# Selective scan with one pass's inputs made on TensorE and a third output product on GpSimd

## The chip, the cores and the metric

The kernel runs on one core of a Trainium2 chip. The metric is the device time of one execution in microseconds (us). A core has five engines with a queue of instructions each: TensorE (PE, its weight loads shown as PEld), VectorE (DVE), ScalarE (ACT), GpSimd (POOL) and SyncE (SP), which here only issues transfers. They wait for one another by semaphores. SBUF is the on-chip memory; PSUM is the memory that TensorE writes and that GpSimd can't reach.

## The reference, cut to what matters

One block of a model on a sequence of 512 tokens of 512 channels: cross attention to a context of 8192 tokens, then a Mamba block with a gated MLP, then a mixture of experts. The change touches only the selective scan of the Mamba block:

```
delta = softplus(dt @ dt_proj_w.T + dt_proj_b)      # [512 tokens, 1024 channels]
A = -exp(A_log)                                     # [1024, 16 states]
def step(h, t):
    dA  = exp(delta_t[..., None] * A)
    dBx = (delta_t * x_t)[..., None] * B_t[:, None, :]
    h = dA * h + dBx
    y = einsum('bdn,bn->bd', h, C_t)
y = ys + xin * D
out = (y * silu(z)) @ out_proj_w.T
```

Everything here is float32, and channels lie on the 128 partitions.

## The kernel before, in words

`mamba_scan` works through 8 blocks of 128 channels (index f) and in each through 8 passes of 2 states (index q): 64 passes, numbered i. A pass has 2 x 512 elements per partition. Its steps:

- u = delta x xin for the block (128 x 512), once per block, on GpSimd (L1385) from the second block on.
- Inputs b = u x B: one product of 128 x 1024 on GpSimd (L1392) into a ring of RB = 3 buffers. B (`bb`) and C (`cc`) lie in SBUF, broadcast to all partitions. The very first is VectorE's (L1448).
- Decays: ScalarE sets the first column to 0 (L1405) and writes exp(delta x A) for each of the two states (L1408) into PSUM, `hs`, a ring of RS = 2.
- Scan: VectorE's tensor_tensor_scan (L1455), h = decay x h + input over the 1024 elements. It writes the states over the decays in PSUM, or, for the passes in `POOL_OUT` (1 and 4), into the SBUF buffer `hc`, ring of RC = 3.
- Output product h x C into `hc`: VectorE (L1462), for passes 1 and 4 GpSimd in place (L1380). GpSimd issues it after the inputs of two passes later.
- Sum: TensorE adds both states of `hc` into the PSUM bank `yp` by matmuls with the identity (L1516). The bank opens with the skip term xin x D (`xk`, L1513, made by ScalarE at L1414). At the end of a block VectorE multiplies the bank by silu(z) (`gate`, L1440), which it does after scan and product of pass 0 of the next block, and TensorE later does the out-projection (L1049), after the sum of pass 7 of the next block.

What sets the order: each engine runs its own list in the order of the code. VectorE's scan i waits for b (`b_ready`), for the decays (`da_ready`), and for the sum of pass i - 3 (`summed`, since the buffer of `hc` is used again). ScalarE's decays i wait until the states of pass i - 2 have been read: by VectorE's product, or for a pass of `POOL_OUT` by the scan alone (`wait_states`). GpSimd's product b waits for the scan of three passes before. TensorE's sums stand in order of i and wait for the product's engine (`wait_outputs`). In the first block ScalarE also does the Silu of z, after the decays of pass 3 (L1417). In the last block some out-projections stand after the sums of passes 2, 3 and 5 (`LAST_AT`).

Of the kernel before, what the change touches and what calls it, by code (L numbers as in the profile page):

```python
# [17 lines left out]
ALU = mybir.AluOpType  # L18
ACT = mybir.ActivationFunctionType
AX = mybir.AxisListType  # L20

P = 128
T = 512
D = 512
TT = T // P
# [1038 lines left out]
HN = 2  # L1064
PASSES = DS // HN

NOW_Z = 2

POOL_OUT = (1, 4)


def scan_rows(keep, first):
# [219 lines left out]
def mamba_scan(nc, keep, n2w, xd_dram, wpack, wsplit):  # L1292
# [6 lines left out]
    with ExitStack() as ctx:  # L1299
# [4 lines left out]
        b = [m.sb(f"b{i}", [P, HN, T]) for i in range(RB)]  # L1304
        hc = [m.sb(f"hc{i}", [P, HN, T]) for i in range(RC)]
        xk = m.sb("xk", [P, 2, T])
        squares = m.sb("squares", [P, 2, T])

        halves_of = lambda a, b: [t[:, 2 * (j % 4):2 * (j % 4) + 2, :].rearrange("p c n -> p (c n)").bitcast(F32)
                                  for j in range(DIC) for t in ((a, b)[j // 4],)]  # L1310
# [26 lines left out]
        block = ctx.enter_context(nc.Block())  # L1337
        passes = [(f, q) for f in range(DIC) for q in range(PASSES)]
        NP = len(passes)

        def pool_passes(n):
            return n // PASSES * len(POOL_OUT) + sum(q in POOL_OUT for q in range(n % PASSES))

        def wait_states(eng, i):

            if i % PASSES in POOL_OUT:
                eng.wait_ge(scanned, i + 1)
            else:
                eng.wait_ge(dve_hc, i + 1 - pool_passes(i))
# [7 lines left out]
        @block.sync  # L1357
        def _(sp):
            for q in range(PASSES):
                sp.dma_start(cc[q], xd_dram[DS + q * HN:DS + (q + 1) * HN, :].partition_broadcast(P)).then_inc(c_in[q], 16)  # L1360
            for n, place in enumerate((keep.hidden, keep.outl)):
                sp.dma_start(place.rearrange("p c n -> p (c n)").bitcast(F32),
                             wpack[W.OUT[0] + n:W.OUT[0] + n + 1, :, :].rearrange("o p n -> (o p) n")).then_inc(w_in, 16)
            sp.dma_start(nw[:, :], n2w).then_inc(n_in, 16)

            sp.wait_ge(b_ready, NP - 1)
            load_gates(sp, keep, wsplit, slice(0, DF // 2), next_in, (0,))
            sp.wait_ge(dve_hc, NP - pool_passes(NP))
            sp.wait_ge(pool_hc, pool_passes(NP))
            load_gates(sp, keep, wsplit, slice(0, DF // 2), next_in, (1,))  # L1370
            sp.wait_ge(next_in, 64)

        @block.gpsimd
        def _(pool):
            def output(i):
                q = i % PASSES
                pool.wait_ge(scanned, i + 1)
                if i < PASSES:
                    pool.wait_ge(c_in[q], 16)
                nc.gpsimd.tensor_tensor(hc[i % RC][:, :, :], hc[i % RC][:, :, :], cc[q], ALU.mult).then_inc(pool_hc, 1)  # L1380

            for i, (f, q) in enumerate(passes):
                if q == 0 and f:
                    pool.wait_ge(b_ready, i - 1)
                    nc.gpsimd.tensor_tensor(u[:, :], keep.delta[:, f, :], keep.xin[:, f, :], ALU.mult).then_inc(u_ready, 1)  # L1385
                    pool.wait_ge(u_ready, f)
                if i >= RB:
                    pool.wait_ge(scanned, i - RB + 1)
                if i == 1:
                    pool.wait_ge(first_ready, 1)  # L1390
                if i:
                    nc.gpsimd.tensor_tensor(b[i % RB][:, :, :], u[:, :].unsqueeze(1).to_broadcast([P, HN, T]),  # L1392
                                            bb[q], ALU.mult).then_inc(b_ready, 1)
                if i >= RB - 1 and (i - RB + 1) % PASSES in POOL_OUT:
                    output(i - RB + 1)
            for i in range(NP - RB + 1, NP):
                if i % PASSES in POOL_OUT:
                    output(i)

        @block.scalar  # L1400
        def _(act):
            for i, (f, q) in enumerate(passes):
                if i >= RS:
                    wait_states(act, i - RS)
                nc.scalar.activation(hs[:, i % RS, :, 0], zero[:, :], ACT.Copy)  # L1405
                for n in range(HN):
                    s = q * HN + n
                    last = nc.scalar.activation(hs[:, i % RS, n, 1:], keep.delta[:, f, 1:], ACT.Exp,  # L1408
                                                scale=aneg[:, f, s:s + 1])
                last.then_inc(da_ready, 1)  # L1410
                if q == 0:
                    if f >= 2:
                        act.wait_ge(summed, PASSES * (f - 2) + 1)
                    nc.scalar.activation(xk[:, f % 2, :], keep.xin[:, f, :], ACT.Copy,  # L1414
                                         scale=dk[:, f:f + 1]).then_inc(xk_ready, 1)
                if i == 3:
                    nc.scalar.activation(keep.zs[:, NOW_Z:, :], keep.zs[:, NOW_Z:, :], ACT.Silu).then_inc(zs_ready, 1)  # L1417

            nc.scalar.activation(rows.sd[:, 0:HN], zero[:, :], ACT.Sqrt).then_inc(warm, 1)
            act.wait_ge(warm, 1)  # L1420
            for t in range(TT):
                act.wait_ge(sum_ready, t + 1)
                if t >= 2:
                    act.wait_ge(ss_ready, t - 1)
                nc.scalar.activation(squares[:, t % 2, :], keep.a[:, t, :], ACT.Square,
                                     accum_out=ss[:, t:t + 1]).then_inc(ss_ready, 1)
            act.wait_ge(var_ready, 1)
            nc.scalar.activation(rows.sd[:, :], rows.var[:, :], ACT.Sqrt).then_inc(sd_ready, 1)
            act.wait_ge(nws_ready, 1)
            for c in range(DC):  # L1430
                act.wait_ge(hT_ready, c + 1)
                nc.scalar.activation(keep.hh[:, c, :], hT[c], ACT.Copy, scale=nws[:, c:c + 1]).then_inc(hh_ready, 1)

        @block.vector
        def _(dve):
# [6 lines left out]
            for i, (f, q) in enumerate(passes):  # L1442
                h = hs[:, i % RS, :, :]
                flat = h.rearrange("p n t -> p (n t)")
                if i:
                    dve.wait_ge(b_ready, i)
                else:
                    nc.vector.tensor_tensor(b[0][:, :, :], u[:, :].unsqueeze(1).to_broadcast([P, HN, T]),  # L1448
                                            bb[0], ALU.mult).then_inc(first_ready, 1)
                    dve.wait_ge(first_ready, 1)  # L1450
                dve.wait_ge(da_ready, i + 1)
                if i >= RC:
                    dve.wait_ge(summed, i - RC + 1)
                out = hc[i % RC][:, :, :]
                nc.vector.tensor_tensor_scan((out if q in POOL_OUT else h).rearrange("p n t -> p (n t)"), flat,  # L1455
                                             b[i % RB].rearrange("p n t -> p (n t)"), 0.0,
                                             ALU.mult, ALU.add).then_inc(scanned, 1)
                if q not in POOL_OUT:
                    dve.wait_ge(scanned, i + 1)
                    if f == 0:  # L1460
                        dve.wait_ge(c_in[q], 16)
                    nc.vector.tensor_tensor(out, h, cc[q], ALU.mult).then_inc(dve_hc, 1)  # L1462
                if q == 0 and f:
                    gate(f - 1)
                if f == DIC - 1 and q == 1:
                    dve.wait_ge(early_ready, 1)
                    nc.vector.tensor_tensor(keep.a[:, 0, :], early, keep.a[:, 0, :], ALU.add).then_inc(early_read, 1)
# [24 lines left out]
        def _(pe):  # L1492
            def out_proj(j, ts):

                pe.wait_ge(y_ready, j + 1)
                for t in ts:
# [8 lines left out]
                    if j == DIC - 1:  # L1505
                        last.then_inc(o_ready, 1)

            for i, (f, q) in enumerate(passes):
                if q == 0:
                    if f:  # L1510
                        pe.wait_ge(y_ready, f)
                    pe.wait_ge(xk_ready, f + 1)
                    nc.tensor.matmul(yp[:, :], ident[:, :], xk[:, f % 2, :], start=True, stop=False)  # L1513
                wait_outputs(pe, i)
                for n in range(HN):
                    last = nc.tensor.matmul(yp[:, :], ident[:, :], hc[i % RC][:, n, :],  # L1516
                                            start=False, stop=(q == PASSES - 1 and n == HN - 1))
                last.then_inc(summed, 1)
                if q == 7 and f:
                    if f == 1:  # L1520
                        pe.wait_ge(w_in, 32)
                    out_proj(f - 1, range(TT - 1) if f - 1 < EARLY else range(1, TT))
                if f == DIC - 1 and q in LAST_AT:
                    pe.wait_ge(early_read, 1)
                    for j in LAST_AT[q]:
                        out_proj(j, (TT - 1,))
# [816 lines left out]
```

## Time and profile before

| what | value |
|---|---|
| median of 3 runs | 2522.21 us (2520.57 to 2522.47) |
| profiled execution, its own time | 2526.3 us |
| its span, first to last instruction | 2524.4 us |
| mean granted TensorE clock | 0.983 |
| the scan stage, from its first instruction to the last gate | 1879.6 to 2091.3 us |
| busy, whole span: PE, DVE, ACT, POOL | 2398.6, 1974.6, 1601.7, 669.9 us |

A busy time counts instructions of an engine from start to end. The granted clock of TensorE is a share of 2.4 GHz; 0.50 is 1.2 GHz. A timeline row merges neighbouring instructions of one line: start, time that they cover, engine, line, operation, out<-in, shapes, count; the bracket is the idle time of the engine before it and who ended it.

### The profile page before, as it was taken

The numbers are of one execution on the slowest core, as the hardware profiler recorded it, in microseconds if no ns is written. First come the engines' busy times: TensorE is split into PE (matmuls) and PEld (weight loads), VectorE is DVE, ScalarE is ACT, GpSimd is POOL, SyncE is SP. The second block draws the span as 40 slices with busy tenths as digits, with TensorE's granted clock in tenths as the row PEclk, the third lists the DMA queues.
The fourth block names the chain that finished last, engine by engine and source line by source line (L and its number), as shares of the span: only waits on it lengthen the run. The fifth ranks groups of instructions, "written<-read, shape, count | busy, mean of one in ns | idle before, by whom it ended". The sixth has DMA issues, their size and how long they took to land. (4 is left out here: it accounts for less than half of the span.)

```text
span 2524.4 us, 39338 instructions
## 1 busy us (share of the span) xinstructions
PE 2398.6 (95%) x14111; PEld 1016.1 (40%) x14111; DVE 1974.6 (78%) x1972; ACT 1601.7 (63%) x1974; POOL 669.9 (27%) x461
## 2 busy tenths in 40 slices
PE   7999999999999799999999999999887778989998
PEld 3333333333333244444444444444332234444554
DVE  5777777777777788888988898988679993267996
ACT  5555555565555478777778877778384442237994
POOL 1455555555555400000000000000019990020001
PEclk9999999999999899999999999999989999999999
DMA  6245654455445593433334333433240005148994
GB/s 250 84 151 164 204 164 150 158 173 167 150 137 157 137 264 81 114 100 98 104 88 110 90 104 88 112 97 95 102 158 22 0 0 200 50 176 317 406 406 171
DMA packets 178206, 366.02 MB, mean 145 GB/s; under 512 B 19546, under 2 KB 90330, under 8 KB 174426
## 3 DMA queue, kind: packets, MB, share of 16 engines
q1 hardware_dynamic: 176610, 360.81, 44.8%
q0 software_dynamic: 1280, 4.20, 0.5%
q8 instruction: 38, 0.62, 0.1%
q14 instruction: 30, 0.24, 0.0%
q10 hardware_dynamic: 248, 0.15, 0.0%
HBM read 254.24 MB, written 106.68 MB: 143 GB/s over the span
## 5 line engine op out<-in xcount | busy, mean ns | idle before, releaser
L466 DVE TENSOR_REDUCE kv_mx<-kv_s 128x1024 f32 (+1 forms) x512 | 595.3, 1217 | 223.7 <-PE kv_s L502 223.7
L818 DVE TENSOR_TENSOR at_pl<-at_pf,at_ph 128x1024 f16<-128x1024 f32 x512 | 613.1, 1223 | 115.6 <-ACT at_ph L765 106.7
L771 ACT ACTIVATE at_pf<-at_st 128x1024 f32<-128x1024 f32 x512 | 497.3, 1025 | 190.3 <-PE at_st L939 137.5
L938 PE MATMUL at_st<-keep_big,at_k_cur 128*128 (+1 forms) x1024 | 390.6, 381 | 10.1 <-DMA keep_big<-q_dram 7.3
L939 PE MATMUL at_st<-keep_big,at_k_one 128*128 (+1 forms) x1024 | 389.1, 380 | 0.0
L765 ACT ACTIVATE at_ph<-at_pf 128x1024 f16<-128x1024 f32 x256 | 272.9, 1066 | 0.0
L1135 POOL MEMSET mamba_zero<- 128x2 f32 x1 | 0.1, 99 | 943.7 <-POOLq L60 943.7
L900 PE MATMUL at_acc<-at_ph,at_vs 128*128 128x512 f16 x1024 | 243.0, 380 | 3.4 <-DVE at_pl L818 3.3
L382 POOL TENSOR_TENSOR kv_ksl<-kv_kf,kv_ksh 128x512 f16<-128x512 f32 x128 | 147.9, 1156 | 247.4 <-ACT kv_ksh L410 247.4
L1049 PE MATMUL kv_kp<-first_ch,first_wkh 128*128 128x512 f16 x512 | 195.4, 382 | 6.1 <-DVEq L448 6.1
L407 ACT ACTIVATE kv_kf<-kv_kp,first_bks 128x512 f32<-128x512 f32 x128 | 87.3, 682 | 172.6 <-PE kv_kp L1049 172.6
L1049 PE MATMUL kv_kp<-first_ch,first_wkl 128*128 128x512 f16 x512 | 195.4, 382 | 0.0
L1049 PE MATMUL kv_kp<-first_cl,first_wkh 128*128 128x512 f16 x512 | 195.1, 381 | 0.0
L1049 PE MATMUL kv_vp<-first_wvh,first_ch 128*128 128x512 f16 x512 | 194.7, 380 | 0.3 <-DVE kv_mx L466 0.3
L1049 PE MATMUL kv_vp<-first_wvl,first_ch 128*128 128x512 f16 x512 | 194.6, 380 | 0.0
L1049 PE MATMUL kv_vp<-first_wvh,first_cl 128*128 128x512 f16 x512 | 194.2, 379 | 0.0
L414 ACT ACTIVATE kv_vf<-kv_vp 128x512 f32<-128x512 f32 x128 | 76.0, 594 | 184.8 <-PE kv_vp L1049 184.8
L386 POOL TENSOR_TENSOR kv_vs<-kv_vf,kv_vs 128x512 f16<-128x512 f32 x128 | 147.9, 1155 | 130.0 <-ACT kv_vs L416 130.0
L814 DVE CAST at_ph<-at_pf 128x1024 f16<-128x1024 f32 x256 | 177.6, 694 | 0.0
L1516 PE MATMUL ms_yp<-ms_hc,keep_ident 128*128 128x512 f32 x256 | 131.7, 655 | 47.6 <-POOL ms_hc L1380 32.7
L938 PEld LDWEIGHTS at_st<-keep_big,at_k_cur 128*128 128x128 f16 x1024 | 100.2, 98 | 171.9 <-issue 54.8
L1392 POOL TENSOR_TENSOR ms_b<-mamba_u,keep_big 128x1024 f32<-128x1024 f32 x63 | 146.4, 2351 | 55.5 <-DVE ms_b L1448 55.0
(349 smaller groups left out, 3863.3 us busy)
## 6 DMA issues: line engine op xcount, KB each, us to landing
keep_big<-gate_up SPq DMA_DIRECT2D x17, 2048.0 KB, 13.0
at_vs<-vd SPq DMA_DIRECT2D x64, 512.0 KB, 3.9
at_k_cur<-kd SPq DMA_DIRECT2D x126, 256.0 KB, 3.8
vd<-kv_vs SPq DMA_DIRECT2D x15, 2048.0 KB, 7.7
kv_tf<-wpack SPq DMA_DIRECT2D x21, 1024.0 KB, 6.3
keep_big<-down SPq DMA_DIRECT2D x17, 1024.0 KB, 14.0
first_cf<-ctxT SPq DMA_DIRECT2D x16, 1024.0 KB, 12.2
ex_yg<-gate_up SPq DMA_DIRECT2D x8, 2048.0 KB, 13.6
```

What stands on the lines that cost most here:

```text
L382: nc.gpsimd.tensor_tensor(ksl[par][:, n, :], kf[:, n % 4, :], ksh[par][:, n, :], ALU.subtract).then_inc(kl_ready, 1)
L386: nc.gpsimd.tensor_tensor(vs[par][:, hs, kt, DH:2 * DH], vf[:, n % 4, :].rearrange("p (h d) -> p h d", d=DH), vs[par][:, hs, kt, 0:DH], AL ...
L466: nc.vector.reduce_max(mx[:, bass.ds(g * (NH * TT) + 2 * (m - TT), 2)], s1[:, m % 3, :, :], AX.X).then_inc(s1_max, 1)
L765: nc.scalar.activation(ph[:, s % RING, :, :], pf[:, s % FULL, :, :], ACT.Copy).then_inc(ph_ready, 1)
L771: nc.scalar.activation(pf[:, s % FULL, :, :], st[:, s % HP % NST, :, :], ACT.Exp, scale=SCORE).then_inc(pf_ready, 1)
L814: nc.vector.tensor_copy(ph[:, s % RING, :, :], pf[:, s % FULL, :, :]).then_inc(ph_own, 1)
L818: nc.vector.tensor_tensor(pl[:, s % RING, :, :], pf[:, s % FULL, :, :], ph[:, s % RING, :, :], ALU.subtract).then_inc(pl_ready, 1)
L900: nc.tensor.matmul(acc[:, 0, :], vs[:, 2 * s + e, :], ph[:, s % RING, e, :], start=(s == 0 and e == 0), stop=False)
L938: nc.tensor.matmul(st[:, w % NST, e, :], k_cur[:, tile], qh[:, q], start=True, stop=False)
L939: last = nc.tensor.matmul(st[:, w % NST, e, :], k_one[:, tile], ql[:, q], start=False, stop=True)
L1049: last = nc.tensor.matmul(out, a, b, start=(start and n == 0), stop=(stop and n == len(pairs) - 1))
L1392: nc.gpsimd.tensor_tensor(b[i % RB][:, :, :], u[:, :].unsqueeze(1).to_broadcast([P, HN, T]), bb[q], ALU.mult).then_inc(b_ready, 1)
```

## The change

- `POOL_OUT` becomes (1, 4, 6): the output product of pass 6 goes from VectorE to GpSimd, and its scan writes `hc`.
- Pass 7 (`TE_PASS`) of each block has its inputs made by TensorE, in PSUM, and no longer by GpSimd. `turn(f)`: four transposes write u of the block, turned, into the half of a state buffer of pass 3 (`TURN_AT`) before its decays go there; ScalarE copies it to SBUF (`uT`). `inputs(f)`: eight matmuls of 128 x 128 x 128 with `uT` as weights and `dg`, B's two rows of pass 7 on diagonals, as the moving side write u x B into `hs`. `turn` stands in TensorE's order ahead of the sum of pass 1, `inputs` ahead of the sum of pass 4.
- The decays of pass 7 go to an SBUF buffer `da`. Its scan reads decays from SBUF and inputs from PSUM.
- VectorE makes `dg` once, by two products after the scan of pass 2.
- GpSimd's and VectorE's counts of `b_ready` leave pass 7 out; GpSimd waits for `turned` before it writes the next u; the squares of the row norm after the scan use the buffer `xk`.

```diff
-POOL_OUT = (1, 4)
+POOL_OUT = (1, 4, 6)
+TE_PASS, TURN_AT = 7, 3
...
-        squares = m.sb("squares", [P, 2, T])
+        squares = xk
+        uT, dg, da = m.sb("uT", [P, TT, P]), m.sb("dg", [P, HN, TT, P]), m.sb("da", [P, HN, T])
...
+        def pool_inputs(n):
+            return n // PASSES * (PASSES - 1) + min(n % PASSES, TE_PASS)
...
 # sync
-            sp.wait_ge(b_ready, NP - 1)
+            sp.wait_ge(b_ready, pool_inputs(NP) - 1)
...
 # gpsimd
-                    pool.wait_ge(b_ready, i - 1)
+                    pool.wait_ge(b_ready, pool_inputs(i) - 1)
+                    pool.wait_ge(turned, f)
...
-                if i >= RB:
-                    pool.wait_ge(scanned, i - RB + 1)
+                k = pool_inputs(i)
+                if q != TE_PASS and k >= RB:
+                    pool.wait_ge(scanned, ITS_PASS[k - RB] + 1)
...
-                if i:
-                    nc.gpsimd.tensor_tensor(b[i % RB][:, :, :], u[:, :].unsqueeze(1).to_broadcast([P, HN, T]),
+                if i and q != TE_PASS:
+                    nc.gpsimd.tensor_tensor(b[k % RB][:, :, :], u[:, :].unsqueeze(1).to_broadcast([P, HN, T]),
                                             bb[q], ALU.mult).then_inc(b_ready, 1)
...
 # scalar
-                if i >= RS:
+                if q == TE_PASS:
+                    if f:
+                        act.wait_ge(scanned, i - PASSES + 1)
+                elif i >= RS:
                     wait_states(act, i - RS)
-                nc.scalar.activation(hs[:, i % RS, :, 0], zero[:, :], ACT.Copy)
+                if q == TURN_AT:
+                    act.wait_ge(turned, f + 1)
+                    if f:
+                        act.wait_ge(in_ready, f)
+                    nc.scalar.activation(uT.rearrange("p t d -> p (t d)"), hs[:, i % RS, 0, :], ACT.Copy).then_inc(uT_ready, 1)
+                    act.wait_ge(uT_ready, f + 1)
+                decays = da if q == TE_PASS else hs[:, i % RS, :, :]
+                nc.scalar.activation(decays[:, :, 0], zero[:, :], ACT.Copy)
...
 # vector
-                if i:
-                    dve.wait_ge(b_ready, i)
+                if q == TE_PASS:
+                    dve.wait_ge(in_ready, f + 1)
+                elif i:
+                    dve.wait_ge(b_ready, pool_inputs(i))
...
+                if q == TE_PASS:
+                    decays, inputs = da.rearrange("p n t -> p (n t)"), flat
+                else:
+                    decays, inputs = flat, b[pool_inputs(i) % RB].rearrange("p n t -> p (n t)")
...
+                if i == 2:
+                    for n in range(HN):
+                        nc.vector.tensor_tensor(dg[:, n, :, :], bb[TE_PASS][:, n, :].rearrange("p (t c) -> p t c", c=P),
+                                                ident[:, :].unsqueeze(1).to_broadcast([P, TT, P]),
+                                                ALU.mult).then_inc(dg_ready, 1)
...
 # tensor
+            def turn(f):
+                i = f * PASSES + TURN_AT
+                wait_states(pe, i - RS)
+                if f:
+                    pe.wait_ge(u_ready, f)
+                for t in range(TT):
+                    last = nc.tensor.transpose(hs[:, i % RS, 0, t * P:(t + 1) * P], u[:, t * P:(t + 1) * P], ident[:, :])
+                last.then_inc(turned, 1)
+
+            def inputs(f):
+                i = f * PASSES + TE_PASS
+                wait_states(pe, i - RS)
+                pe.wait_ge(uT_ready, f + 1)
+                if f == 0:
+                    pe.wait_ge(dg_ready, HN)
+                for t in range(TT):
+                    for n in range(HN):
+                        last = nc.tensor.matmul(hs[:, i % RS, n, t * P:(t + 1) * P], uT[:, t, :], dg[:, n, t, :],
+                                                start=True, stop=True)
+                last.then_inc(in_ready, 1)
...
             for i, (f, q) in enumerate(passes):
+                if q == TURN_AT - 2:
+                    turn(f)
+                if q == TE_PASS - 3:
+                    inputs(f)
```

## Rows read from the trace of the kernel before

**Rows 1.** Stretches: engine, busy us and count in 26 us of the scan; PEclk, DMA.

```profile
1956.00:1982.00 26.00, 19.52 (x44) 7.60 (x43) 25.79 (x16) 12.05 (x27) 24.68 (x12) 1.00 0.00 0
```

**Rows 2.** Timeline, VectorE, one block: start us, us, engine, line, operation, count.

```profile
1961.49 1.22 DVE L1462 TENSOR_TENSOR ms_hc<-ms_hs,keep_big 128x1024 f32<-128x1024 f32 x1
...
1962.63 0.68 DVE L1440 TENSOR_TENSOR mamba_yh<-ms_yp,mamba_zs 128x512 f32<-128x512 f32 x1
...
1963.23 2.28 DVE L1455 TENSOR_TENSOR_SCAN ms_hc<-ms_hs,ms_b 128x1024 f32<-128x1024 f32 x1
...
1965.43 2.27 DVE L1455 TENSOR_TENSOR_SCAN ms_hs<-ms_hs,ms_b 128x1024 f32<-128x1024 f32 x1
...
1967.73 1.22 DVE L1462 TENSOR_TENSOR ms_hc<-ms_hs,keep_big 128x1024 f32<-128x1024 f32 x1
...
1968.88 2.29 DVE L1455 TENSOR_TENSOR_SCAN ms_hs<-ms_hs,ms_b 128x1024 f32<-128x1024 f32 x1
...
1987.23 1.22 DVE L1462 TENSOR_TENSOR ms_hc<-ms_hs,keep_big 128x1024 f32<-128x1024 f32 x1
```

**Rows 3.** Groups by line, GpSimd, one block: count, busy us, mean ns, idle.

```profile
L1392 POOL TENSOR_TENSOR ms_b<-mamba_u,keep_big 128x1024 f32<-128x1024 f32 x9 | 20.9, 2352 | 0.1
...
L1385 POOL TENSOR_TENSOR mamba_u<-mamba_delta,mamba_xin 128x512 f32<-128x512 f32 x1 | 1.3, 1266 | 0.1
```

**Rows 4.** Timeline, GpSimd, its first product with C; in brackets idle before, releaser.

```profile
1965.59 2.34 POOL L1380 TENSOR_TENSOR ms_hc<-ms_hc,keep_big 128x1024 f32<-128x1024 f32 x1 [1.16 <-DVE ms_hc L1455]
```

**Rows 5.** Tile of the output sum: the matmul records of L1516.

```profile
L1516 PE MATMUL ms_yp<-ms_hc,keep_ident x256: 592/592/1223, 1884.7 to 2090.0; 128*128 128x512 f32 x128
```

**Rows 6.** Timeline, TensorE, sums of passes 0 and 1 before.

```profile
1964.56 1.88 PE L1516 MATMUL ms_yp<-ms_hc,keep_ident 128*128 128x512 f32 x4
...
1965.42 0.19 PEld L1516 LDWEIGHTS ms_yp<-ms_hc,keep_ident 128*128 128x128 f32 x1 [0.24 <-issue]
```

**Rows 7.** Timeline, last sum and final gate of the scan.

```profile
2088.60 1.98 PE L1516 MATMUL ms_yp<-ms_hc,keep_ident 128*128 128x512 f32 x4 [0.81 <-DVE ms_hc L1462]
...
2090.62 0.69 DVE L1440 TENSOR_TENSOR mamba_yl<-ms_yp,mamba_zs 128x512 f32<-128x512 f32 x1 [2.08 <-PE ms_yp L1516]
```

**Rows 8.** Timeline, float32 transposes of 128 columns: full clock, then 1.2 GHz.

```profile
2304.21 0.57 PEld L2183 LDWEIGHTS ex_up<-keep_ident,ex_smf 128*128 128x128 f32 x4
...
2304.43 0.60 PE L2183 MATMUL ex_up<-keep_ident,ex_smf 128*128 128x128 f32 x4
...
2102.27 2.42 PEld L1533 LDWEIGHTS ms_hs<-keep_ident,ms_hc 128*128 128x128 f32 x12 [5.65 <-issue]
```

**Rows 9.** Timeline, TensorE, pass 4's sum in the block f = 2.

```profile
1951.47 4.97 PE L1516 MATMUL ms_yp<-ms_hc,keep_ident 128*128 128x512 f32 x7 [2.75 <-POOL ms_hc L1380]
...
1952.42 0.34 PEld L1516 LDWEIGHTS ms_yp<-ms_hc,keep_ident 128*128 128x128 f32 x1 [0.52 <-issue]
```

**Rows 10.** Stretch in that sum, with its granted clock (PEclk).

```profile
1952.00:1953.00 1.00, 1.00 (x2) 0.34 (x1) 1.00 (x2) 0.64 (x2) 1.00 (x1) 0.50 0.00 0
```

**Rows 11.** Lines L1157 (ScalarE reads PSUM) and L1225 (VectorE, both inputs in SBUF).

```profile
L1157 ACT ACTIVATE mi_xp<-mi_zp x8: 578/581/598, 1830.1 to 1849.1; 128x512 f32<-128x512 f32 x8
...
L1225 DVE TENSOR_TENSOR mamba_u<-mamba_delta,mamba_xin x1: 682/682/682, 1877.5 to 1877.5; 128x512 f32<-128x512 f32 x1
```

**Rows 12.** Timeline, ScalarE, zero column and decays of one pass.

```profile
1962.75 0.17 ACT L1405 ACTIVATE ms_hs<-mamba_zero 128x2 f32<-128x2 f32 x1 [2.07 <-DVE ms_hc L1462]
...
1962.86 1.28 ACT L1408 ACTIVATE ms_hs<-mamba_delta,mamba_aneg 128x511 f32<-128x511 f32 x2
```

**Rows 13.** Timeline, first block: sum 0, decays of passes 3 and 4, scan 4.

```profile
1884.72 3.78 PE L1516 MATMUL ms_yp<-ms_hc,keep_ident 128*128 128x512 f32 x4 [0.98 <-DVE ms_hc L1462]
...
1887.01 1.28 ACT L1408 ACTIVATE ms_hs<-mamba_delta,mamba_aneg 128x511 f32<-128x511 f32 x2
...
1893.73 1.30 ACT L1408 ACTIVATE ms_hs<-mamba_delta,mamba_aneg 128x511 f32<-128x511 f32 x2
...
1895.11 2.29 DVE L1455 TENSOR_TENSOR_SCAN ms_hc<-ms_hs,ms_b 128x1024 f32<-128x1024 f32 x1 [1.34 <-ACT ms_hs L1408]
```

More of the change, by code:

```diff
@@ L1306, in mamba_scan @@
         xk = m.sb("xk", [P, 2, T])
-        squares = m.sb("squares", [P, 2, T])
+        squares = xk
+        uT, dg, da = m.sb("uT", [P, TT, P]), m.sb("dg", [P, HN, TT, P]), m.sb("da", [P, HN, T])
+        turned, uT_ready, dg_ready, in_ready = (m.sem(n) for n in ("turned", "uT_ready", "dg_ready", "in_ready"))
         halves_of = lambda a, b: [t[:, 2 * (j % 4):2 * (j % 4) + 2, :].rearrange("p c n -> p (c n)").bitcast(F32)
@@ L1339, in mamba_scan @@
         NP = len(passes)
+        ITS_PASS = [i for i, (f, q) in enumerate(passes) if q != TE_PASS]
         def pool_passes(n):
             return n // PASSES * len(POOL_OUT) + sum(q in POOL_OUT for q in range(n % PASSES))
+        def pool_inputs(n):
+            return n // PASSES * (PASSES - 1) + min(n % PASSES, TE_PASS)
         def wait_states(eng, i):
@@ L1402, in _ @@
             for i, (f, q) in enumerate(passes):
-                if i >= RS:
+                if q == TE_PASS:
+                    if f:
+                        act.wait_ge(scanned, i - PASSES + 1)
+                elif i >= RS:
                     wait_states(act, i - RS)
-                nc.scalar.activation(hs[:, i % RS, :, 0], zero[:, :], ACT.Copy)
+                if q == TURN_AT:
[6 more added lines that the diff above has]
+                nc.scalar.activation(decays[:, :, 0], zero[:, :], ACT.Copy)
                 for n in range(HN):
                     s = q * HN + n
-                    last = nc.scalar.activation(hs[:, i % RS, n, 1:], keep.delta[:, f, 1:], ACT.Exp,
+                    last = nc.scalar.activation(decays[:, n, 1:], keep.delta[:, f, 1:], ACT.Exp,
                                                 scale=aneg[:, f, s:s + 1])
@@ L1454, in _ @@
                 out = hc[i % RC][:, :, :]
-                nc.vector.tensor_tensor_scan((out if q in POOL_OUT else h).rearrange("p n t -> p (n t)"), flat,
-                                             b[i % RB].rearrange("p n t -> p (n t)"), 0.0,
-                                             ALU.mult, ALU.add).then_inc(scanned, 1)
+                if q == TE_PASS:
+                    decays, inputs = da.rearrange("p n t -> p (n t)"), flat
+                else:
+                    decays, inputs = flat, b[pool_inputs(i) % RB].rearrange("p n t -> p (n t)")
+                nc.vector.tensor_tensor_scan((out if q in POOL_OUT else h).rearrange("p n t -> p (n t)"), decays, inputs,
+                                             0.0, ALU.mult, ALU.add).then_inc(scanned, 1)
+                if i == 2:
[3 more added lines that the diff above has]
+                                                ALU.mult).then_inc(dg_ready, 1)
                 if q not in POOL_OUT:
```

## The prediction

> **What bounds the kernel now.** I read the table of stretches first. In the 26 us stretch of the scan stage VectorE is busy 25.79 us and GpSimd 24.68, ScalarE 12.05 [rows 1]: VectorE has no gap, GpSimd a little, ScalarE half. So the scan's time is what VectorE issues, and only what VectorE does or waits for counts. The timeline of one block of 128 channels (f = 3 into f = 4) gives its cadence, start to start [rows 2]: a scan and its multiply 3.45 us (1965.43 to 1968.88: scan 2.30, multiply 1.15), a scan whose output GpSimd multiplies 2.20 (1963.23 to 1965.43), the gate multiply 0.60. One block is 6 x 3.45 + 2 x 2.20 + 0.60 = 25.7 us, and the rows of the two multiplies with C at 1961.49 and 1987.23 are 25.74 apart. Eight blocks are the stage, from 1879.6 to the last gate.
>
> GpSimd makes per block eight products u x B of 2.35 us, one u of 1.27 [rows 3] and two products with C of 2.34; before the first of these it sits idle 1.16 us, waiting for a scan [rows 4]. At 2.3 us start to start its own work is 24.6 us.
>
> **The change, part by part.**
>
> *Removed.* VectorE no longer multiplies pass 6: 3.45 becomes 2.25; with the shorter handover of a scan that follows a scan, 2.20. That is 1.26 us less per block, 10.1 in eight. GpSimd exchanges one product of 2.35 for one of 2.34, so its 24.6 stay. If VectorE ran free at 25.74 - 1.26 = 24.5, GpSimd's 24.6 would be the bound, and the gain at most 1.1 per block.
>
> *Added on TensorE, and its place.* This is the step that decides. Inputs of pass 7 are eight plain float32 products of 128 columns, issued ahead of pass 4's sum in TensorE's program. They wait until VectorE has multiplied pass 5, since they overwrite that state. Queued behind them is the sum of pass 4, and the scan of pass 7 waits for this sum as well (the ring of three outputs: pass 7 needs passes 0 to 4 summed). In the kernel before, pass 4 is summed as soon as GpSimd has its product, well ahead of need. Now a chain runs from the end of pass 5's multiply: 0.06 to start, the eight products, the sum of 1.98, 0.04 to VectorE. Beside it runs only the scan of pass 6: by the cadence scan 7 could start 2.12 us after pass 5's multiply ends (multiply 1.22 long, next scan 1.14 after its start, next one 2.20 later). The old multiply of pass 6, which would have covered 1.26 more, is gone.
>
> How long are the eight? The view by tile lists 256 matmul records for the 128 sums' matmuls [rows 5]: a plain float32 matmul is two records, so sixteen records of 128 columns. For 512 columns a record takes 0.427 us (four in 1.88 with a tail of 0.17; the sum takes 1.98 in all [rows 6, 7]). By columns 128 are 0.107, the lower bound: 1.7 us for sixteen. Upper bound: a weight load of 0.19 [rows 6] not hidden at all, 0.30 each, 4.8 us. The nearest rows are float32 transposes: four loads in 0.57 with 0.14 the last, 0.143 apart, at the full clock; twelve in 2.42, 0.20 apart, with the clock at 1.2 GHz [rows 8]. A plain load record is longer (0.19 against 0.14). I take 0.17 at 2.4 GHz: 2.7 us. The stall of scan 7 is 0.06 + 2.7 + 1.98 + 0.04 - 2.12 = 2.7 us.
>
> The clock makes it worse. Before its sum of pass 4 TensorE sits idle 2.75 us, and the granted clock falls to 0.50 (1.2 GHz) right there: at 1951.8 it starts the sum and the rows after it show 0.50 and loads of 0.34 [rows 9, 10]. The same fall stands at this place in five of the eight blocks (0, 2, 4, 5, 6), some 3.5 us each. The new wait is at this place, idle longer still (until pass 5's multiply), so I let five of eight groups of products run at 1.2 GHz, with the 0.17 stretched as the transposes' 0.143 to 0.20: 0.24, sixteen 3.8 us, stall 3.8; the sum behind it again at 2.4. Together 3 x 2.7 + 5 x 3.8 = 27.1 us.
>
> *The rule on loads.* The loads of the sums start while the previous matmul streams and are followed by 0.24 us of waiting [rows 6]: hidden. The Trainium skill, "TensorE: Matmul & The Clock Gate", Part 3, "The mechanism", says the opposite for full-height tiles: a weight load overlaps matmuls in flight only if the row groups differ. Its "LDWEIGHTS" section gives 128 columns / 1.2 = 107 ns; an estimate from this page is 0.107 + 0.107 per record, a stall of 3.4 in each block, and by that a sum of 22 us where my 2.7 gives 16, both with the clock up. The rows speak against it for long matmuls and show nothing for plain short ones.
>
> *Turning u.* Four transposes between the sums of pass 0 and 1, then ScalarE copies them out of PSUM, waits for its own copy, and only then makes the decays of pass 3. Before, these could begin at the end of scan 1. Counted from the gate's start G = 1962.63: TensorE is busy with out-projection, the skip term and sum 0 until G + 3.64 (last record 1965.42 + 0.43, the rest being the pipeline), so the transposes end at G + 4.27 (0.60 for four [rows 8]); copy 0.58 [rows 11], own wait 0.04; zero column to first decay 0.11, decays 1.28 [rows 12]: ready at G + 6.35. Scan 3 starts at G + 6.25 (1968.88). So 0.1 per block, 0.6 in the six blocks that have an out-projection there; ScalarE's idle half covers the rest. Without that cover each further microsecond would be one of stall.
>
> *First block.* With the clock at 1.2 GHz sum 0 takes 3.78 us from 1884.72, its stream ending at 1888.1 [rows 13]; transposes 1.0, copy 0.6, and decays of pass 3 end at 1891.2 instead of 1888.3. Behind them ScalarE has the Silu of z with its table loads; so pass 4's decays end at 1897.9 instead of 1895.03, and scan 4, which already waits for them (1.34 idle), starts 2.8 later. The two diagonal products of VectorE (128 x 512, both inputs in SBUF, 0.68 each [rows 11]) lie inside these 2.8 and cost nothing more. Without that cover the two would cost VectorE 1.3.
>
> *Last block.* Sum 5, an out-projection of two matmuls, sum 6 and sum 7 are four times 1.71 behind the late sum 4, so the final gate, which waits 2.08 for sum 7 today [rows 7], waits about 1.2 more.
>
> *At nothing:* decays of pass 7 into SBUF (ScalarE need not wait for a state any more; it runs them right after pass 6's); the extra semaphores; the earlier weight load on SyncE's queue (bytes that the next stage needs 10 us later); the shared buffer of squares (used after the scan). GpSimd's wait for the turn ends long before it computes u. GpSimd's third product with C ends about as sum 4 does and its sum is needed only by the gate some 7 us later.
>
> **Sum:** -10.1 + 27.1 + 0.6 + 2.8 + 1.2 = +21.6 us. The profiled execution took 2526.3 (its span 2524.4), 4.1 above the median of 2522.2; the difference laid on the median gives 2543.8. A block should last 25.74 - 1.26 + 2.7 or 3.8 + 0.1 = 27.3 to 28.4.
>
> **Rivals.**
> A. The loads of short float32 matmuls are not hidden: 0.30 each hot, stall 4.8; cold 0.34 + 0.21 = 0.55, stall 8.8. All hot: -10.1 + 38.4 + 4.6 = +33, 2555; with the five falls +53, 2575. For it: nothing here streams short plain float32 products. Against: hidden loads in the rows of the sums, and transposes at less than load plus stream. The Trainium skill's rule quoted above is this rival's mechanism.
> B. The products cost half: one record each as the sixteen transposes have (0.107, 0.86 in all): stall 0.8, sum -10.1 + 6.6 + 4.6 = +1.1, 2523: no change. Against: two records per plain matmul.
> C. Faster: sum 4 does not hold scan 7, because the products are done before VectorE gets there, and GpSimd's 24.6 sets the block: 8 x -1.14 + 2.8 + 0.6 = -5.7, 2516.5. It decides from the point where sixteen records and the sum fit into 2.12 us; as the sum alone is 1.98, this needs TensorE's order or waits to be other than I read them. Break-even is at (10.1 - 4.6) / 8 = 0.7 us of stall.
> That the change doesn't do what it says, with the output of pass 6 left on VectorE, I see no sign of.
>
> **Chances.** Forecast 0.67, A 0.15, B 0.08, C 0.10. The forecast's own range: records at 0.107 and no falls give +8 (2530), all eight at 1.2 GHz and 0.19 for 0.17 give +29: 2530 to 2551. The range for 8 in 10 takes in B's edge and A's lower part: 2522 to 2560. What can be told from no change is 0.2%, 5 us. Slower 0.82, same 0.08, faster 0.10.
>
> **What would show it.** VectorE idle before the scan of pass 7 in every block, released by TensorE's sum, 2.5 to 4 us each; sixteen short records right ahead of the four of sum 4; a block of 27.3 to 28.4; GpSimd with 3 us idle per block; scan 4 of the first block near 1898. Wrong if scan 7 follows scan 6 at 2.20 us, if the eight products take under 1 us, or if GpSimd is the engine without gaps.

## The result, and the profile after

The changed kernel takes 2549.87 us (median of 5 runs, 2547.78 to 2551.99) against 2522.47 before (5 runs): ratio 1.0102, 95% interval 1.0091 to 1.0113, slower by 27.4 us. 2543.8 was predicted, with 2522 to 2560 as the range. The profiled executions took 2550.1 and 2526.3, 23.8 apart; the one of before lay 3.8 above its median, the one of after on it. I measure by the stage, from VectorE's first product to the final gate: 211.0 us before (1879.60 to 2090.62), 234.2 after (1878.75 to 2112.99), so 23.2 of the 23.8 are in it. Blocks, gate to gate, last 27.9 to 28.2 us in four cases, 29.3 in two and 26.8 in the last one; before they last 25.7, and 25.0 the last one.

VectorE's waits in the stage after the change (who waited for whom: us in total, times, longest), the answer to [rows 2]; before, VectorE had none ahead of the scan of pass 7:

```profile
DVE ms_hs L1483 <- PE ms_yp L1573: 27.6, 8, 4.6
DVE mamba_yl L1462 <- PE ms_yp L1573: 3.2, 1, 3.2
```

And the timeline of VectorE in one block: scan 5, its multiply, scan 6, scan 7.

```profile
1983.56 2.27 DVE L1483 TENSOR_TENSOR_SCAN ms_hs<-ms_hs,ms_b 128x1024 f32<-128x1024 f32 x1
1985.87 1.23 DVE L1494 TENSOR_TENSOR ms_hc<-ms_hs,keep_big 128x1024 f32<-128x1024 f32 x1
1987.01 2.28 DVE L1483 TENSOR_TENSOR_SCAN ms_hc<-ms_hs,ms_b 128x1024 f32<-128x1024 f32 x1
1993.88 2.30 DVE L1483 TENSOR_TENSOR_SCAN ms_hs<-ms_da,ms_hs 128x1024 f32<-128x1024 f32 x1 [4.59 <-PE ms_yp L1573]
```

Scan 6 follows pass 5's multiply by 1.14 as before; scan 7 should follow 2.20 later, at 1989.2, and starts at 1993.88. TensorE in the same stretch, the answer to [rows 9]: sixteen short records, then the sum of pass 4 (merged here with the next one); and the same two in the last block.

```profile
1987.15 3.78 PE L1557 MATMUL ms_hs<-ms_dg,ms_uT 128*128 128x128 f32 x16 [3.66 <-DVE ms_hc L1494]
1990.72 3.46 PE L1573 MATMUL ms_yp<-ms_hc,keep_ident 128*128 128x512 f32 x5
```

```profile
2102.31 2.05 PE L1557 MATMUL ms_hs<-ms_dg,ms_uT 128*128 128x128 f32 x16 [1.88 <-DVE ms_hc L1494]
2104.20 3.17 PE L1573 MATMUL ms_yp<-ms_hc,keep_ident 128*128 128x512 f32 x7
```

The stretches (PE busy, PEld, DVE, ACT, POOL, then PEclk) say why the first took 3.78 us and the other 2.05:

```profile
1988.00:1989.00 1.00, 1.00 (x6) 1.00 (x6) 1.00 (x1) 0.00 (x0) 1.00 (x1) 0.50 0.00 0
1992.00:1993.00 1.00, 1.00 (x2) 0.34 (x1) 0.00 (x0) 0.00 (x0) 1.00 (x2) 0.50 0.00 0
2103.00:2104.00 1.00, 1.00 (x12) 1.00 (x11) 1.00 (x1) 0.10 (x1) 0.00 (x0) 1.00 1.05 377
```

At 1.2 GHz the sum too is slow: from 1990.72 to 1993.88 it is 3.2 us instead of 2.0. The granted clock fell at this place in seven of the eight blocks. TensorE sat idle 3.6 to 3.7 us before the products in these seven and 1.9 us in the last, where the clock stayed up. In four of the seven it fell in the idle time (in the block shown at 1986.2), in three of them 0.4 to 1.3 us after the products had begun. VectorE's wait before scan 7 follows it: 1.76 us with the clock up, 3.15 to 3.44 in the five blocks where it was down for some 3.5 us, 4.53 and 4.59 in the two where it was down for some 7.

### The profile page after: what moved, and what is told of

It reads as the page before. It is cut to its first block and busy times, and to the rows that moved or that the text cites. A ratio compares the mean times of both kernels' runs of the same rounds, so it can differ in the third digit from the quotient of the medians.

```text
span 2548.2 us, 39690 instructions
## 1 busy us (share of the span) xinstructions
PE 2422.2 (95%) x14271; PEld 1042.7 (41%) x14271; DVE 1969.9 (77%) x1966; ACT 1607.3 (63%) x1982; POOL 672.9 (26%) x461
## 5 line engine op out<-in xcount | busy, mean ns | idle before, releaser
L900 PEld LDWEIGHTS at_acc<-at_ph,at_vs 128*128 128x128 f16 x1024 | 99.9, 98 | 124.4 <-DVE at_pl L818 4.5
L1403 POOL TENSOR_TENSOR ms_b<-mamba_u,keep_big 128x1024 f32<-128x1024 f32 x55 | 129.2, 2369 | 73.1 <-DVE ms_b L1472 56.3
```

The costliest lines, as they stand in the source:

```text
L900: nc.tensor.matmul(acc[:, 0, :], vs[:, 2 * s + e, :], ph[:, s % RING, e, :], start=(s == 0 and e == 0), stop=False)
L1403: nc.gpsimd.tensor_tensor(b[k % RB][:, :, :], u[:, :].unsqueeze(1).to_broadcast([P, HN, T]), bb[q], ALU.mult).then_inc(b_ready, 1)
```

## The experiments

All times are medians beside runs of the kernel before on the same chip (2522.5 to 2523.9); "stage" as above. The numbers (e1 to e11) are those by which the expectations name one another: "the second experiment" is e2, "the tenth" e10.

**e1: the order of products and sum 4.**

```diff
-                if q == TE_PASS - 3:
+                if q == TE_PASS - 2:
                     inputs(f)
```

> The eight products of pass 7 stand behind the sum of pass 4 in TensorE's order instead of ahead of it; nothing else changes. Theory (the scan of pass 7 waits for a chain of products and sum that starts at the end of pass 5's multiply): sum 4 can now start when GpSimd's product is done, 0.9 us before that multiply ends, so the chain is shorter by that: a wait of scan 7 of 0.9 us where the clock is up and 2.6 where it falls before sum 4, about 16 us in eight blocks where there were 27.6; time about 2538. Rival (GpSimd's third product with C is what is late, the order on TensorE doesn't matter): the waits stay at 3 to 4 us, time 2550.

2535.1 us, ratio 1.0045 (1.0028 to 1.0062); stage 220.6. The waits before scan 7 fell by half and name the products now, no sum:

```profile
DVE ms_hs L1483 <- PE ms_hs L1557: 13.5, 8, 2.4
```

So 13.7 us of the stage were one line of order: the chain is shown. Part of them came by the clock: like with like, the wait is 0.64 us for 1.76 with the clock up and about 2.3 for 3.3 with it down, some 1.1 us per block either way; the rest is that the clock now fell at this place in five blocks, not seven, and never for 7 us.

**e3: the length of the products.** In `inputs`, `for n in range(HN)` becomes `for n in range(1)`. This kernel leaves out half of the inputs of pass 7.

> Leaves out four of the eight products of each block (the second state of pass 7 keeps what was in PSUM). Theory with length in it: 0.94 us less per block with the clock up, 1.8 with it down, the sum of the waits before scan 7 falls from 27.6 to 14 to 18 us, time about 2537. Rival (the wait is a matter of order and handovers, the length of the products is small beside it): under 4 us less.

```profile
DVE ms_hs L1483 <- PE ms_yp L1573: 16.5, 8, 2.5
```

2538.4 us in its one run, near the 2537 expected. 11.1 us of waiting less for eight times eight records less is 0.17 us each, but some of it is the clock again, which fell at this place in six blocks and never for 7 us. In the last block, at full clock in both kernels, the wait is 0.87 for 1.76: 0.11 us a record.

**e7: the clock.** `none` holds zeros, written by GpSimd at the start (that line isn't shown).

```diff
             def inputs(f):
                 i = f * PASSES + TE_PASS
+                if f == 0:
+                    pe.wait_ge(none_ready, 1)
+                for n in range(4):
+                    nc.tensor.matmul(yp[:, :], none[:, :], cc[0][:, 0, :], start=False, stop=False)
                 wait_states(pe, i - RS)
```

> Four matmuls of 512 columns with zero weights are added into the output sum just ahead of TensorE's wait for pass 5's multiply (3.4 us of work in an idle time of 3.7), so that TensorE isn't idle before the products. Theory: the granted clock stays at 2.4 GHz through products and sum 4, sixteen records take 1.9 us as in the one block where it was up, each wait is 1.8 us as there, sum about 15 us where it was 27.6; time 2537. Rival (the clock is no part of it, the products are slow by themselves): waits stay at 3 to 4.5 us, time 2550 or, with the filler late, more.

2536.5 us, ratio 1.0049 (1.0032 to 1.0065), stage 223.7. Waits and, in one block, the products:

```profile
DVE ms_hs L1487 <- PE ms_yp L1581: 15.4, 8, 3.1
```

```profile
1955.30 2.05 PE L1565 MATMUL ms_hs<-ms_dg,ms_uT 128*128 128x128 f32 x16 [0.23 <-DVE ms_hc L1498]
```

With work ahead of them the products run as in the last block of the changed kernel (2.05 us), and 12.2 of 27.6 us of waiting are gone, though TensorE does more; the stage is 10.5 shorter. Seven of the eight waits are now 1.76 us, that of the block whose clock had stayed up; in the last block the wait grew to 3.1, as the added work (3.4 us) is longer than TensorE's idle time there (1.9). The granted clock is 1.00 in all eight groups of products and the sums behind them. So of the time lost at this place nearly half was the granted clock, and TensorE's idle time before the products was what brought it down.

**e5, one part alone: the inputs on TensorE.** `POOL_OUT` back to (1, 4).

> The changed kernel with pass 6's output product back on VectorE (two passes on GpSimd as before), inputs of pass 7 still on TensorE. Theory: the 1.26 us per block of that product now lie beside TensorE's products and sum 4 and cover them; the waits of scan 7 shrink by as much, from 27.6 to about 18 us in all, and the time is that of the changed kernel within a few us: 2547 to 2552. That would say that moving the product to GpSimd bought nothing here. Rival (each part has its own cost or gain, the move gains 10 us by itself): 2560.

2549.8 us, ratio 1.0106 (1.0089 to 1.0123), no different from the changed kernel's. The waits:

```profile
DVE ms_hs L1483 <- PE ms_yp L1573: 17.3, 8, 3.3
```

10.3 us less than 27.6, which is the 10.1 of work that came back. The product's move to GpSimd bought nothing: it uncovered the wait.

**e4, one part alone: the third product on GpSimd.** The kernel before with `POOL_OUT = (1, 4, 6)`.

> The kernel before with the output product of pass 6 on GpSimd and nothing else: GpSimd makes all eight inputs and three output products. Theory (work of GpSimd's list, 8 x 2.32 + 3 x 2.30 + 1.45): GpSimd has 26.9 us of work per block and becomes the bound, blocks of 26.9 to 27.2 instead of 25.74, stage from 211.0 to about 221, time 2532. Rival (VectorE's released time counts, GpSimd keeps up through its rings): blocks of 24.5 to 25, time 2515.

2543.9 us, ratio 1.0078 (1.0061 to 1.0094), stage 232.6; both theories missed. VectorE waits, at the gates:

```profile
DVE mamba_yh L1440 <- PE ms_yp L1516: 17.0, 4, 4.7
DVE mamba_yl L1440 <- PE ms_yp L1516: 15.2, 4, 4.7
```

GpSimd's work, 26.9 us per block, is part of it; the rest is order: its product of pass 6 stands behind u and the next block's first inputs, sums 6 and 7 come after it, and the gate waits up to 4.7 us. Behind the late gate stands the scan of pass 1, and for this GpSimd in turn sits idle, 1.54 or 2.78 us by turns:

```profile
1973.30 2.35 POOL L1380 TENSOR_TENSOR ms_hc<-ms_hc,keep_big 128x1024 f32<-128x1024 f32 x1 [1.54 <-DVE ms_hc L1455]
```

26.87 and these give the blocks of 28.4 and 29.6 us that alternate here.

**e6: four output buffers.** `RB, RC, RS = 3, 4, 2`.

> The changed kernel with four output buffers instead of three, so that the scan of pass 7 needs passes 0 to 3 summed and no longer pass 4. Theory: only the products themselves (1.9 us with the clock up, about 3.6 down, and 0.3 of latency) can hold scan 7, beside 2.12 of cover: waits of 0.1 to 1.9, 8 to 12 us in all instead of 27.6; time 2530 to 2534. Rival (the sum behind the products doesn't matter, scan 7 waits for the products anyway): waits stay above 20 us, 2545 or more.

2543.0 us, ratio 1.0077 (1.0060 to 1.0094); stage 227.7. Its waits:

```profile
DVE ms_hs L1483 <- PE ms_hs L1557: 8.5, 7, 1.7
DVE ms_hs L1483 <- ACT ms_hs L1430: 5.9, 5, 1.4
DVE mamba_yl L1462 <- PE ms_yp L1573: 5.0, 1, 5.0
...
DVE mamba_yh L1462 <- PE ms_yp L1573: 3.0, 4, 1.0
DVE ms_hs L1483 <- POOL ms_b L1403: 2.1, 2, 1.4
```

The products hold scan 7 for 8.5 us in all, as expected of the one wait. The time missed the expectation by 10 us: once scan 7 isn't late, sums 4 to 7, the out-projection and the turning of u are still late on TensorE. They hold the gates (8.0 us, 5.0 of it the last one) and, by the decays of pass 3, scan 3 (1.4 us in each of four blocks). Taking one wait away moved VectorE into the next.

**e2: pass 6 on TensorE.** `TE_PASS = 6`, products behind sum 3.

> Pass 6 instead of pass 7 gets its inputs from TensorE; the state that these overwrite is pass 4's, which is free as soon as scan 4 ends, since GpSimd multiplies that pass; the products stand behind sum 3. Theory: scan 5 and its multiply (3.45 us) now cover the products (1.9 us with the clock up, 3.6 with it down), so VectorE's waits before that scan nearly vanish (under 0.5 us each, 0.2 in most), a block lasts about GpSimd's 24.6 to 24.9 us instead of 28.3, and the time is 2517 to 2523, on either side of the kernel before. Rival (GpSimd with three products with C, or short products on TensorE as such, cost the time): blocks stay above 27 us and the time above 2540.

2555.3 us, ratio 1.0127 (1.0110 to 1.0144), stage 245.4: the slowest of all. Where I had aimed, the theory holds; scan 5, its multiply and scan 6 follow without a gap:

```profile
1985.14 2.27 DVE L1483 TENSOR_TENSOR_SCAN ms_hs<-ms_hs,ms_b 128x1024 f32<-128x1024 f32 x1
...
1987.45 1.22 DVE L1494 TENSOR_TENSOR ms_hc<-ms_hs,keep_big 128x1024 f32<-128x1024 f32 x1
...
1988.59 2.27 DVE L1483 TENSOR_TENSOR_SCAN ms_hc<-ms_da,ms_hs 128x1024 f32<-128x1024 f32 x1
```

But the gates wait 34 us in all:

```profile
DVE mamba_yh L1462 <- PE ms_yp L1573: 16.9, 4, 4.8
DVE mamba_yl L1462 <- PE ms_yp L1573: 16.9, 4, 4.7
```

The reason is GpSimd's list (inputs of pass 7, u, inputs of pass 0, product of pass 6):

```profile
1957.81 2.36 POOL L1403 TENSOR_TENSOR ms_b<-mamba_u,keep_big 128x1024 f32<-128x1024 f32 x1
1960.25 1.27 POOL L1395 TENSOR_TENSOR mamba_u<-mamba_delta,mamba_xin 128x512 f32<-128x512 f32 x1
1961.59 2.34 POOL L1403 TENSOR_TENSOR ms_b<-mamba_u,keep_big 128x1024 f32<-128x1024 f32 x1
1963.90 2.34 POOL L1389 TENSOR_TENSOR ms_hc<-ms_hc,keep_big 128x1024 f32<-128x1024 f32 x1
```

Scan 6 ended at 1961.07; its product starts at 1963.90, after u and the inputs. Time and blocks (up to 30.7 us) are as the rival has them, but not by its cause: with the same three products in another order, in e9, they aren't.

**e9: the same with GpSimd's list put right.** It makes the inputs of pass 7 before it multiplies pass 4:

```diff
-                if i >= RB - 1 and (i - RB + 1) % PASSES in POOL_OUT:
-                    output(i - RB + 1)
+                late = i - (3 if q == PASSES - 1 else 2)
+                if q != TE_PASS and late >= 0 and late % PASSES in POOL_OUT:
+                    output(late)
```

> Pass 6 gets its inputs from TensorE behind sum 3, as in the second experiment, and GpSimd makes the inputs of pass 7 before it multiplies pass 4 by C (there it sat idle 3.6 us waiting for scan 4, and its product of pass 6 came so late that the gate waited 3.7 to 4.8 us per block, 33.8 in all). Theory: product of pass 6 ends about 8.4 us after scan 4, sums 6 and 7 at 12.2, the gate is due at 12.6: the gate's waits fall under 1 us where the clock is up, blocks take 24.6 to 25.2, stage about 205, time 2516 to 2520, faster than the kernel before. Rival (the gate waits because sums 6 and 7 run at 1.2 GHz or stand behind other work of TensorE): waits of 2 us and more remain, blocks above 26, time above 2528.

2527.9 us (ratio 1.0017, 1.0007 to 1.0027), 27 us better than without it, stage 213.3; blocks of 25.7, not 24.6, so it isn't faster than the kernel before, though I had expected that. Only the first gate (1.3 us) and the last (2.9) still wait. What was left is in neither theory: scan 3 waits 1.13 to 1.26 us in five blocks for the decays behind the copy of u.

```profile
1968.94 0.60 PE L1547 MATMUL ms_hs<-keep_ident,mamba_u 128*128 128x128 f32 x4
...
1969.62 0.60 ACT L1425 ACTIVATE ms_uT<-ms_hs 128x512 f32<-128x512 f32 x1 [3.86 <-DVE ms_hs L1484]
...
1971.73 2.30 DVE L1484 TENSOR_TENSOR_SCAN ms_hs<-ms_hs,ms_b 128x1024 f32<-128x1024 f32 x1 [1.15 <-ACT ms_hs L1431]
```

**e10: the out-projection later**, so that TensorE turns u earlier: blocks 2 to 6 do it behind the sum of pass 2.

> As the last experiment of pass 6 on TensorE with GpSimd's new order, and in blocks 2 to 6 the out-projection stands behind the sum of pass 2 instead of behind the sum of pass 7 of the block before. There TensorE's turning of u came after the out-projection, and scan 3 waited 1.15 us per block for decays behind the copy of u. Theory: turned u is there 2.6 us earlier, that wait goes in five blocks, blocks of 24.55 to 24.7 (GpSimd's 24.6), stage from 213.3 to about 208, time 2520 to 2522. Rival (the wait comes from ScalarE's own order, copy and its wait before the decays, whatever TensorE does): blocks stay at 25.7, time 2527.

2522.6 us, ratio 0.9997 (0.9988 to 1.0006): no change against the kernel before. The stage is 209.7, not 208. The wait at scan 3 is gone in the five blocks, and GpSimd is the engine without gaps in the middle ones: its inputs of pass 0 in two following blocks are 24.44 apart. Two of the seven blocks still last 26.0 us: there the granted clock fell to 0.50 in sums 6 and 7, and the gate behind them waits 1.46.

```profile
1957.34 2.35 POOL L1403 TENSOR_TENSOR ms_b<-mamba_u,keep_big 128x1024 f32<-128x1024 f32 x1
...
1981.78 2.35 POOL L1403 TENSOR_TENSOR ms_b<-mamba_u,keep_big 128x1024 f32<-128x1024 f32 x1
```

**e8: the diagonal products.**

> The changed kernel with the two diagonal products of VectorE at the very start of the scan, while GpSimd still waits for its first buffer, instead of after scan 2, where they took 2.13 us each. Theory (they are slow because GpSimd works beside them on SBUF while both their inputs are in SBUF): 0.68 us each here. Rival (their access pattern, a row against an identity repeated four times, is slow by itself): 2.1 each here too. The stage's start is later by the products' time either way; time 2550 to 2552.

2551.0 us in one run. Each product takes 0.69 us here, so the theory holds and their access pattern isn't what is slow. By tile (ns: least, median, greatest), in the changed kernel and here:

```profile
L1487 DVE TENSOR_TENSOR ms_dg<-keep_big,keep_ident x2: 1514/2170/2827, 1888.4 to 1889.8; 128x512 f32<-128x512 f32 x2
```

```profile
L1465 DVE TENSOR_TENSOR ms_dg<-keep_big,keep_ident x2: 684/688/691, 1877.5 to 1878.1; 128x512 f32<-128x512 f32 x2
```

**e11: first block.** On top of e10, the turn of block 0 goes before pass 5, and `dg` reads the identity from PSUM.

> The tenth experiment, and in the first block u is turned before pass 5 and not before pass 3, so that ScalarE's Silu isn't behind the copy; and the diagonal products read the identity from PSUM (a transpose of TensorE puts it there), so one of their inputs only is in SBUF, with GpSimd working beside them. Theory: diagonal products of 0.68 us instead of 2.13, scan 4 of the first block 2.5 to 3.3 us earlier, some 0.6 given back at scan 5: stage about 205.5, time 2518 to 2520. Rival (their access pattern is slow by itself): 2.1 each, scan 4 is then bound by them, time as in the tenth.

```profile
L1490 DVE TENSOR_TENSOR ms_dg<-keep_big,ms_op x2: 674/674/674, 1887.8 to 1888.4; 128x512 f32<-128x512 f32 x2
```

```profile
1893.98 2.29 DVE L1485 TENSOR_TENSOR_SCAN ms_hc<-ms_hs,ms_b 128x1024 f32<-128x1024 f32 x1 [0.29 <-ACT ms_hs L1432]
```

With GpSimd working beside them and one input in PSUM the products take 0.67 us, and scan 4 starts 15.6 us into the stage, where it was 18.4 in e10, as expected.

2520.0 us, ratio 0.9991 (0.9982 to 1.0000), stage 206.4, 4.6 below the kernel before. The stage is clearly shorter; of the whole the runs can't tell more than 0 to 0.2%. It is the best version, and no clear win.

## Why the prediction was right

- *The deciding step held*: products, then sum 4, then scan 7, from the end of pass 5's multiply. Waits of 27.6 us (28.2 with the handover, 0.08 more each) against 27.1 predicted. That the sum came so close is luck: two errors cancel. Products at the full clock were cheaper: (2104.20 - 2102.31) / 16 = 0.118 us a record, near my lower bound of 0.107, where I took 0.17. The clock fell in seven blocks, not five, and stayed down for some 7 us in two of them, so that sum 4 ran slow as well; I had given the falls to the products alone. Against my 3 x 2.7 + 5 x 3.8 stand 1 x 1.76, five waits of 3.15 to 3.44 and two of 4.5: no single block waited what I said, and two blocks of 29.3 us and the last of 26.8 lie outside my 27.3 to 28.4. I also read the fall of the clock before the change as coming ahead of the sum of pass 4, with the sum starting at 1951.8; the row has it start at 1951.47, and the clock fell at 1951.6.
- *Removed work*: 10.1. Without its wait the block after the first lasts 27.97 - 3.41 - 0.08 = 24.48 (from 1908.50 to 1936.47).
- *Turning u*: 0.1 predicted in six blocks (the terms add up to G + 6.28, not 6.35), 0.2 measured in five: in the last block VectorE has an addition to do ahead of scan 2, and nothing waits. In the five, scan 3 starts 1.34 after the multiply and not 1.14, behind the decays:

```profile
1975.78 0.60 ACT L1424 ACTIVATE ms_uT<-ms_hs 128x512 f32<-128x512 f32 x1 [2.82 <-issue]
...
1976.52 1.28 ACT L1430 ACTIVATE ms_hs<-mamba_delta,mamba_aneg 128x511 f32<-128x511 f32 x2
1976.55 1.22 DVE L1494 TENSOR_TENSOR ms_hc<-ms_hs,keep_big 128x1024 f32<-128x1024 f32 x1
...
1977.89 2.30 DVE L1483 TENSOR_TENSOR_SCAN ms_hs<-ms_hs,ms_b 128x1024 f32<-128x1024 f32 x1
```

- *First block*: 2.8 predicted; scan 4 starts 18.4 us into the stage instead of 15.5, so 2.9. ScalarE's chain did what was forecast (decays ready at 1896.92), but the diagonal products took 4.3 us and not 1.4. VectorE has no gap from them to scan 4, so they alone made scan 4 as late. With them out of the way, in e8, scan 4 waits 3.2 us for ScalarE and starts as late. That the 2.8 fits is luck too, since I had these products three times too cheap:

```profile
1888.35 4.26 DVE L1487 TENSOR_TENSOR ms_dg<-keep_big,keep_ident 128x512 f32<-128x512 f32 x2
...
1895.62 1.30 ACT L1430 ACTIVATE ms_hs<-mamba_delta,mamba_aneg 128x511 f32<-128x511 f32 x2
...
1897.13 2.28 DVE L1483 TENSOR_TENSOR_SCAN ms_hc<-ms_hs,ms_b 128x1024 f32<-128x1024 f32 x1
```

- *Last gate*: it waits 3.2 instead of 2.1, 1.1 for 1.2 predicted.
- The sum: -10.1 + 28.2 + 1.0 + 2.9 + 1.1 = 23.1, measured 23.2 by the profiles. Between the profiled executions the difference is 23.8, between the medians 27.4. The other 3.6 are that the profiled execution of before lay 3.8 above its median; where in it these lie no trace shows.
- *Rival A* (loads not hidden, 0.30 a record) is refuted by 0.118. The trace doesn't agree with the Trainium skill's sentence in "TensorE: Matmul & The Clock Gate", Part 3, "The mechanism", that weight loads overlap with matmuls in flight only when the row groups differ: the estimate of 0.214 from it is nearly twice what a record took. The same section opens with an exception, a load into a background weight buffer, which the prediction left out. *Rival B* has its two records per product against it (128 records for 64 products). *Rival C* didn't come about, as sum 4 does hold scan 7. What GpSimd would do with VectorE free, e1 comes nearest to showing: its shortest block lasts 25.40 us with 0.64 of waiting before scan 7, and sums 6 and 7 are done at 2017.4, a microsecond before the gate at 2018.41. So the gate waits of 4 us in e2 belong to the list there, where the inputs of pass 7 stand ahead of u as well. That GpSimd's 24.6 would have bounded the changed kernel as it stands was not run; with pass 6 on TensorE and three more edits blocks of 24.44 were reached, 1.3 us below the kernel before.

## What to carry to other kernels

Work that moves to an idle engine costs by what its wait holds back in that engine's queue: before moving, write down the event that it starts from, what is queued behind it, and what cover remains when the move also takes work off the busy engine. Start it from an event that comes early (here a scan instead of a scan and multiply), and order the helper's list by who waits. A wait taken away shows its next one, so count on the gain only after all lists are walked.

## What the runs showed of the hardware

A float32 product on VectorE with both inputs in SBUF took 2.17 us on average for 128 x 512 while GpSimd worked on SBUF, 0.69 while GpSimd was idle, and 0.67 with GpSimd busy and one input in PSUM. GpSimd was slower as well: its two products beside them took 5.55 us instead of 4.65. The Trainium skill, "GPSIMD Engine Reference", section 8, names this contention (shared SBUF interfaces, VectorE instructions with two SBUF inputs); the runs agree and give a factor of three. I had priced these products from a row where GpSimd was idle [rows 11].

A plain float32 matmul of 128 columns ran at 0.118 us per record with its 128 x 128 weight load hidden, at 2.4 GHz, and at about 0.22 (3.57 / 16 in the block shown) at 1.2 GHz. Idle time of TensorE in front of a short critical piece was paid twice here: in seven of eight blocks, after 3.6 to 3.7 us of idle, the granted clock was 0.50 in at least part of that piece, and filling the idle time with matmuls that add zero gave back 12 us of waiting and 10.5 of the stage.
